# A recurrence of 256 steps: gates closed by scans over pairs, input products spread over every step, eight steps in a loop body

## What is computed

```python
def cell(h, x):
    gi = x @ W_ih + b_ih
    gh = h @ W_hh + b_hh
    i_r, i_z, i_n = jnp.split(gi, 3, axis=-1)
    h_r, h_z, h_n = jnp.split(gh, 3, axis=-1)
    r = jax.nn.sigmoid(i_r + h_r)
    z = jax.nn.sigmoid(i_z + h_z)
    n = jnp.tanh(i_n + r * h_n)
    h_new = (1.0 - z) * n + z * h
    return (h_new, h_new)
_, hs = jax.lax.scan(cell, initial_state, xs)
```

## Time and profile before

| | us |
|---|---|
| median of 3 runs | 2221.06 |
| lowest and highest | 2219.84, 2222.62 |
| span of the profiled execution | 2220.2 |
| share of TensorE, VectorE, ScalarE, GpSimd busy | 87%, 61%, 48%, 17% |
| first `sum_r` of the recurrence | at 1262.8 |
| last of them | at 2160.3 |

### The profile page before, as it was taken

How to read it: one execution, slowest core, us unless ns; L and a number is a source line. 1 busy time by engine, 2 the same in 40 slices (tenths; PEclk the granted TensorE clock), 3 DMA queues, 4 the chain that set the end, 5 groups by cost and what they waited for, 6 DMA issues and landing times. The chain is left out here.

```text
span 2220.2 us, 88821 instructions
## 1 busy us (share of the span) xinstructions
PE 1931.2 (87%) x33310; PEld 1399.4 (63%) x33310; DVE 1343.3 (61%) x5503; ACT 1074.6 (48%) x4057; POOL 375.9 (17%) x1399
## 2 busy tenths in 40 slices
PE   6888989879789797898877899999999998989876
PEld 4244455435444454445444788888888898989775
DVE  4648365474374653835634467777777677767766
ACT  0343634626326254263364455555556565656444
POOL 3000000000000000000000133333333333333334
PEclk7699998989899998999988879797979797969556
DMA  8042150320512504216012300000000000000002
GB/s 205 22 66 58 36 114 25 61 65 30 87 35 53 96 28 66 57 33 113 15 67 58 101 0 1 0 0 0 0 0 0 0 0 0 0 0 0 0 0 76
DMA packets 100770, 87.00 MB, mean 39 GB/s; under 512 B 12856, under 2 KB 87736, under 8 KB 100680
## 3 DMA queue, kind: packets, MB, share of 16 engines
q1 hardware_dynamic: 100296, 85.61, 16.9%
q0 software_dynamic: 384, 0.01, 0.0%
HBM read 60.20 MB, written 21.00 MB: 37 GB/s over the span
## 5 line engine op out<-in xcount | busy, mean ns | idle before, releaser
L1059 PE MATMUL bank_pair_A<-moving,rep 128*128 128x16 f16 x8192 | 328.9, 172 | 68.9 <-ACT bank_pair_C L1142 40.5
L1059 PEld LDWEIGHTS bank_pair_A<-moving,rep 128*128 128x128 f16 x8192 | 268.7, 99 | 107.0 <-DVE moving L1284 80.4
L1059 PE MATMUL bank_pair_C<-moving,rep 128*128 128x16 f16 x8192 | 321.8, 171 | 0.0
L1059 PE MATMUL bank_pair_B<-moving,rep 128*128 128x16 f16 x8192 | 321.7, 171 | 0.0
L1059 PEld LDWEIGHTS bank_pair_B<-moving,rep 128*128 128x128 f16 x8192 | 266.4, 99 | 0.0
L1059 PEld LDWEIGHTS bank_pair_C<-moving,rep 128*128 128x128 f16 x8192 | 266.3, 99 | 0.0
L1151 ACT ACTIVATE r_gate<-r_pre 128x8 f32<-128x8 f32 (+1 forms) x512 | 110.5, 216 | 291.9 <-DVE r_pre L1244 252.5
L1046 PE MATMUL bank_pair_D<-x_part,w_in 128*128 128x256 f16 x1536 | 209.0, 284 | 6.0 <-ACT gi_rz L1179 3.4
L939 POOL TENSOR_TENSOR x<-x,w_in 128x512 f32<-128x512 f32 x8 | 10.3, 1288 | 1096.3 <-DMA w_in<-w_in 1096.3
L848 DVE TENSOR_REDUCE head_max<-bank_pair_A 128x2 f32<-128x1024 f32 x128 | 155.7, 1217 | 64.5 <-PE bank_pair_A L440 64.0
L1244 DVE TENSOR_REDUCE r_pre<-bank_pair_A 128x8 f32<-128x16 f32 (+1 forms) x512 | 97.8, 191 | 138.9 <-PE bank_pair_A L1059 119.8
(11 more groups left out here) (237 smaller groups left out, 3611.6 us busy)
## 6 DMA issues: line engine op xcount, KB each, us to landing
rep<-parts SPq DMA_DIRECT2D x64, 256.0 KB, 6.8
parts<-parts SPq DMA_DIRECT2D x48, 256.0 KB, 2.8
q_rep<-parts SPq DMA_DIRECT2D x32, 256.0 KB, 4.0
k_rep<-parts SPq DMA_DIRECT2D x64, 128.0 KB, 2.5
w_in<-in_x_dram SPq DMA_DIRECT2D x8, 512.0 KB, 4.7
x<-in_x_dram SPq DMA_DIRECT2D x8, 512.0 KB, 3.6
w_in<-w_in SPq DMA_DIRECT2D x128, 32.0 KB, 1.9
parts<-parts SPq DMA_DIRECT2D x32, 128.0 KB, 2.5
```

The costliest lines, as they stand in the source:

```text
L1059: last = nc.tensor.matmul(ps[part][:, o:o + 2 * B], w[:, k, (first + c) * P:(first + c) * P + P], moving[:, k, :, :].rearrange("p s b -> p ...
```

## The change

- *Products.* They stand in all 32 steps of a block: six in each step (`PER_STEP`), 48 (three chunks m) in a body of eight steps, alternating between the two banks of `pD`. `x_part` has two buffers, `gi` is one tensor, and GpSimd makes the two parts of x two blocks ahead, 32 elements in a step.
- *Loops.* `blocks` is written out for the 8 blocks, each a loop of four passes over a body of eight steps.
- *Gates.* The tiles hold pairs, batch by batch. With `r_factor` = (0, r) and `n_pair` = (h_n, i_n) a scan (state = factor x state + term) leaves r h_n + i_n in the second place (`gated_n`); with `w_factor` = (0, 1 - z) and `state` = (n - h, h) it leaves the new state (`new_state`, twice). `towards` writes n - h. The n bank is added up without r (`sum_n`).
- *Orders.* The sequences on VectorE and ScalarE are written anew; TensorE waits for the sixth seed and the fifth later.

The core of the diff:

```diff
-        def blocks(eng, step, split, product):
-            with eng.Fori(0, BLOCKS - 1) as blk:
-                with eng.Fori(0, PLAIN // BODY) as k:
...
+        def blocks(eng, step):
+            for blk in range(BLOCKS):
+                with eng.Fori(0, PASSES) as i:
+                    for j in range(STEPS):
+                        step(i * STEPS + (blk * TB + j), j, i, blk)
...
+            def step(step, j, i, blk):
+                pe.wait_ge(seeded, step * 6 + 4)
+                pe.wait_ge(lo_done, step * 2 + 1)
+                for ps, column in ((pR, 0), (pN, 2 * DC), (pZ, DC)):
+                    gate(ps, column, 0, CHUNKS[0])
+                gate(pR, 0, 1, CHUNKS[0])
                 pe.wait_ge(seeded, step * 6 + 5)
...
+                gate(pN, 2 * DC, 1, CHUNKS[0])
+                pe.wait_ge(seeded, step * 6 + 6)
+                gate(pZ, DC, 1, CHUNKS[0])
                 pe.wait_ge(lo_done, step * 2 + 2)
...
+                if blk == BLOCKS - 1:
+                    return
...
+                for n in range(j * PER_STEP, (j + 1) * PER_STEP):
+                    m, at = n // PRODUCTS, n % PRODUCTS
+                    if at == 0:
+                        pe.wait_ge(gi_out, i * PER_PASS + ((blk + 1) * MC + (0, -1, 1)[m]))
+                    last = product(i * PER_PASS + m, at, blk + 1, pG[m % 2])
...
                 gate("r", 0)
-                gate("z", 0)
+                gate("w", 0)
                 seed(step + 1, "r", 0)
+                gate("n", 0)
                 gate("r", 1)
-                gate("n", 0)
+                seed(step + 1, "n", 0)
                 seed(step + 1, "z", 0)
                 seed(step + 1, "r", 1)
-                seed(step + 1, "n", 0)
-                act.wait_ge(n_mul, step * 2 + 2)
+                gate("n", 1)
+                gate("w", 1)
                 seed(step + 1, "n", 1)
-                gate("n", 1)
-                gate("z", 1)
                 seed(step + 1, "z", 1)
...
+                if blk < BLOCKS - 1:
+                    for m in range(PER_PASS):
+                        if j * PER_STEP < (m + 1) * PRODUCTS <= (j + 1) * PER_STEP:
+                            evacuate(blk + 1, i * PER_PASS + m, pG[m % 2])
...
+                def gated_n(part):
...
+                    nc.vector.tensor_tensor_scan(flat(n_pre, part), flat(r_factor, part), flat(n_pair, part), 0.0, ALU.mult, ALU.add).then_inc(n_sum, 1)
...
+                    for out, done in ((hi, hi_done), (new, st_ok)):
+                        nc.vector.tensor_tensor_scan(flat(out, part), flat(w_factor, part), flat(old, part), 0.0, ALU.mult, ALU.add).then_inc(done, 1)
```

More of the change, by code:

```diff
@@ L1003, in halves, with flat, second, first @@
             return ps.rearrange("p (c s b) -> p c b s", s=2, b=B)
-        def blocks(eng, step, split, product):
-            with eng.Fori(0, BLOCKS - 1) as blk:
-                with eng.Fori(0, PLAIN // BODY) as k:
[L1010 to L1024, removed]
+        def flat(pairs, part):
+            return pairs[:, SLICE[part], :, :].rearrange("p c b o -> p (c b o)")
+        def second(pairs, part):
+            return pairs[:, SLICE[part], :, 1:2].rearrange("p c b o -> p c (b o)")
+        def first(pairs, part):
+            return pairs[:, SLICE[part], :, 0:1].rearrange("p c b o -> p c (b o)")
+        def blocks(eng, step):
[3 more added lines that the diff above has]
+                        step(i * STEPS + (blk * TB + j), j, i, blk)
         @block.sync
@@ L1072, in step @@
                 for part in range(2):
[L1073 to L1086 removed]
+                    for ps, column, done in ((pR, 0, r_ps), (pN, 2 * DC, n_ps), (pZ, DC, z_ps)):
+                        gate(ps, column, part, CHUNKS[1]).then_inc(done, 1)
@@ L1091, in first_products @@
                     pe.wait_ge(gi_out, m - 1)
-                for k in range(DC):
-                    if m == 0:
-                        pe.wait_ge(x_lo, k + 1)
-                    last = products(m, k, pG[m % 2])
+                for n in range(PRODUCTS):
+                    if m == 0 and n % 4 == 0:
+                        pe.wait_ge(x_lo, n // 4 + 1)
+                    last = product(m, n, 0, pG[m % 2])
                 last.then_inc(gi_ps, 1)
@@ L1121, in _ @@
                 for part in range(2):
-                    last = nc.tensor.matmul(ps[part], w_part[0][:, 0, 0:P], moving[:, SLICE[part], :, :].rearrange("p c s b -> p (c s b)"),
-                                            start=True, stop=True)
+                    for c in CHUNKS[part]:
+                        o = (c - CHUNKS[part][0]) * 2 * B
+                        last = nc.tensor.matmul(ps[part][:, o:o + 2 * B], w_part[0][:, 0, 0:P],
+                                                moving[:, :, c, :, 1:2].rearrange("p s b o -> p s (b o)"),
+                                                start=(o == 0), stop=True, skip_group_check=True)
             last.then_inc(begun, 1)
-            blocks(pe, step, nothing, product)
+            blocks(pe, step)
         @block.scalar
@@ L1199, in _ @@
             act.wait_ge(zeros, 1)
-            for kind in "rnz":
-                for part in range(2):
+            for part in range(2):
+                for kind in "rnz":
                     seed(0, kind, part)
-            blocks(act, step, nothing, product)
+            blocks(act, step)
         @block.vector
@@ L1276, in new_state @@
                 def new_state(part):
-                    dve.wait_ge(zn_ok, step * 2 + (part + 1))
-                    for out, done in ((moving[:, SLICE[part], 0, :], hi_done), (new[:, SLICE[part], :], st_ok)):
-                        nc.vector.scalar_tensor_tensor(out=out, in0=z_new[:, SLICE[part], :], scalar=-HS, in1=z_old[:, SLICE[part], :],
-                                                       op0=ALU.mult, op1=ALU.add).then_inc(done, 1)
+                    dve.wait_ge(e_ok, step * 2 + (part + 1))
```

232 lines of the change are left out of this document (102 added, 130 removed).

## The result

The changed kernel takes **2371.84 us** (median of 4 runs, 2368.55 to 2373.45) where the kernel before takes 2221.84 beside it: a ratio of 1.0677, with a 95% interval of 1.0662 to 1.0692. Forecast were 2362 us (2270 to 2400) and slower with a chance of 0.88. One of the eleven executions of the second kernel of experiment 5 was slow, at 6095 us, and does not enter its ratio.

A forecast was written before the change was run, and what follows sets the result against it. TensorE was taken to bound steps with products, the dependency chain those without. The 2220.2 us span + 72.9 (clock) + 67.7 (loop body) + 0 gave 2360.8, plus 0.9 around it: 2362 us, range 2270 to 2400.

The forecast's parts named there:

- Clock, +72.9 us: Seven blocks with six products a step: clock stays at 1.2 GHz, TensorE-bound steps of 3.85 us, 72.9 us more.
- the recurrence's slow beginning: Recurrence begins with seed waits and small matmuls, where the clock falls; a reason for taking 1.2 GHz throughout.
- Loop body, +67.7 us: TensorE's eight-step loop body is mostly fetched anew at jumps back, adding 67.7 us; bounds 0 and 83.5 us.
- 20 of 24: Of 24 jumps back in the recurrence's eight loop copies, 20 were taken to wait for instructions.
- 3.48 us each: Cost of each waiting jump back in the recurrence, taken from attention's six jumps, 20.9 us in all.
- VectorE and ScalarE, 0: Gate work hidden behind TensorE in blocks with products; last block's chain about unchanged: 0, bounds -5 and +5 us.
- as walked: The chain followed operation by operation in the new order: 3.50 us a step, where it was 3.48.
- -25.7 us: Other bound of the clock term: seven blocks at 2.4 GHz throughout, chain-bound at 3.41 us a step, 25.7 us less.
- faster: 2195: Rival: clock up and loop body loaded, every step at the chain's 3.41 us, 2195 us in all; chance 0.11.
- Split of x, "hidden": GpSimd's split, one 32-element piece per step, fits within the 3.85 us step and costs nothing extra.
- Evacuations, branches: 0: ScalarE's 12 evacuations a block end before the next gate is due; dropping three loops and their branches saves nothing: 0.

The follow-up runs named there:

- experiment 5: New gates and orders in the loops of the kernel before: 2252.89 us; second kernel, also with VectorE's second-half n sum and scan moved earlier: 2216.74 us.
- experiments 2 and 5: The first of the two: changed kernel, loop copies shifted onto seven packets, plus two wasted wide matmuls a step (2239.23 us) or one (2346.57 us).
- experiment 7: Changed kernel with GpSimd's split early, VectorE reordered, first copies placed on seven packets, two wasted products a step in block 0 alone: 2345.26 us.
- gates-alone kernel: Kernel before with only the new gates and the new VectorE and ScalarE orders, old loops kept: 2252.89 us, ratio 1.0155.

## Why the prediction was right

*Clock, +72.9 us: right, 70.7 measured.* The step is 3.84 us, forecast 3.85, at 0.50 from first to last. The choice of the low clock holds under test: the runs with six and with seven wide matmuls in a step stay low, those with eight rise (and can fall again, experiments 2 and 5), and six after eight fall back. The prediction also leaned on the recurrence's slow beginning; experiment 7 shows that six a step do not keep the clock even when they begin at 1.00.

*Loop body, +67.7 us: the sum right to a tenth, by two errors that cancel.* The forecast was 20 of 24 jumps at 3.48 us. It is 15 at 4.97. What failed is "3.48 us each": in attention one wait stands at a jump, here two, of 2.3 us on average (69.4 / 30). Why attention, whose body touches eight packets as well, waits only once was not tested. And "20 of 24" came from matmul counts between 608 and 860; what decides is whether a copy touches seven or eight packets, which the program's text gives up to one number, where the first packet begins. The Trainium skill's room of 2048 instructions ("Runtime: NRT & Kernel Launch", "Instruction fetch mechanics"), which I weighed against it, is eight packets; the runs show that a body of 1701 stays when it touches seven of them and is read whole in every pass when it touches eight.

*VectorE and ScalarE, 0: right here for the reason given, wrong beside it.* At 3.84 us a step TensorE covers the chain, and the last block's step is 3.50 as walked. The scans are 0.257 us, forecast 0.26, where ordinary operations on as many elements take 0.18 to 0.21. From 16 to 48 elements the scan for `moving` grows from 0.193 to 0.258 us, 2 ns an element, and the r sum from 0.175 to 0.207, 1 ns; the half rate that the Trainium skill gives for the scan ("DVE: opcode table, instruction layouts, handler registers and perf-mode slots", "Datapath and trigger behaviour") agrees. But "-25.7 us" with a chain of 3.41 at 2.4 GHz was wrong: the queue of VectorE makes it 3.49, and 3.55 beside GpSimd's split. The rival "faster: 2195" rested on it. With no waits and the clock mostly up the change's gates gave 2239 us, with two wasted matmuls in each step and the small ones between the copies. Without these, six blocks at 3.55 and one at 3.49 would make 2221 + 192 x 3.55 + 32 x 3.49 - 789.5, some 2225 us, an estimate from the steps of that run; so the rival would not have come out even under its own conditions.

*Split of x, "hidden": wrong by 6.8 us.* I looked at how long the piece takes and not at what stands ahead of it in GpSimd's queue.

*Evacuations, branches: 0, as forecast.* The last block is 0.7 us longer.

The sum gave a span of 2360.8 us, 9.4 less than came: the jumps are 6.8 of it, the first steps 6.8, the last block 0.7; the clock gives back 2.2, and the recurrence's earlier start 2.8.

## What to carry to other kernels

Before spreading an engine's work evenly, look whether the clock was earned by its unevenness: 192 products in 24 steps of eight ran mostly at 2.4 GHz, the same 192 in 32 steps of six ran at 1.2 GHz throughout. When a loop body is unrolled, count the 16 KB packets that it touches from where it lies, not its instructions; one packet more cost 4.6 us at every jump, and small matmuls ahead of the loops, which shift it, removed that. In an in-order queue a shorter operation gains nothing when it stands behind work that could come later: the gates with two operations fewer, and their new orders, made the old loops 32 us slower, and another order of the same operations on VectorE took 36 us off.

## What was unexpected of the hardware

- In the recurrence a jump to a loop that touches eight packets makes two waits, up to 3.4 us each with products and up to 4.7 in steps without (experiment 7; attention, 3.5 us, makes one), and all packets are read anew: 33 on q8 in a block of four passes, against 7 where the copy touches seven.
- Wasted matmuls pay: eight wide ones a step instead of six took 60 us off (2298.9 to 2239.2 us), while seven cost 48 (2346.6).
- On the change from eight wide matmuls a step to six the clock fell from 1.00 to 0.50 within two steps, though TensorE was busy for 6.80 of the 7.00 us before, and it stayed there while TensorE did not pause once (115 us).
- In the gates-alone kernel the scan of 16 elements for `moving` took 0.41 to 0.43 us in the 27 steps in which it ran beside a cast on GpSimd, and 0.19 elsewhere.
